# Retention on one Trainium2 core: when GpSimd prepares the next attention's buffers

## The chip, the cores and the metric

The kernel runs on one core of one Trainium2 chip. The core has five engines that run side by side and meet only at semaphores: TensorE (PE in the profile), VectorE (DVE), ScalarE (ACT), GpSimd (POOL) and SyncE (SP), which here only issues transfers. The metric is the device time of one execution in microseconds, the median of several runs. Three runs before the change took 1232.62, 1233.42 and 1237.57 us.

## The reference

Two decoder layers work on 64 sequences of 64 tokens of width 128, so 4096 tokens. Each layer is three sublayers, each added to its input after a layer norm:

```
x = x + state_space(norm(x))          # layer 0
x = x + attention(norm(x), context)
x = x + mixture_of_experts(norm(x))
x = x + retention(norm(x))            # layer 1
x = x + projected_attention(norm(x), context)
x = x + mixture_of_experts(norm(x))
```

The change lies in the retention, 8 heads with keys of 64 and values of 128:

```
q, k = rotary(x @ Wq.T), rotary(x @ Wk.T)       # per head
v, g = x @ Wv.T, x @ Wg.T
scores = (q @ k.T) * 64**-0.5 * decay[head]     # causal, no softmax
o = scores @ v
o = (o - mean(o)) * rsqrt(var(o) + 1e-5) * gn_weight + gn_bias
out = (o * silu(g)) @ Wo.T
```

The attention after it reads keys and values of the context, which were projected at the start of the program and lie in SBUF as kT and v_twice.

## The kernel before

The program is a row of phases, each one block with a barrier at its end. The tokens stay in SBUF as X, 32 tiles of 128 tokens. `layers` (L2083) runs the retention phase between the first mixture of experts and the attention a1.

`retention_phase` (L989) handles one tile per step. Each engine's instructions are written out by hand in `step(i, k)`, and `skewed` (L42) issues them: the first four steps (eight on ACT) are peeled, with step numbers known as Python integers, then comes a hardware loop of four steps per turn, then the last steps, in which only late stages are live. A `between` callback, where given, is issued after the peeled steps. Different stages of different tiles share a step, so the work of a tile spreads over about five steps.

The way of tile m through the engines, in brackets the line:

- ACT normalises the tile into xn (L1211). PE transposes it (L1309), ACT copies it out as the part x_high (L1200), DVE forms the rest x_low (L1155).
- PE makes q and k of all heads (L1232 to L1236), then v with the same lines. DVE multiplies q and k by cosines into qk (L1118), and their swapped halves by sines into turned (L1129). POOL adds turned to qk (L1073): this ends the rotary embedding.
- PE transposes qk (L1266) once POOL has added. ACT copies the transposes (L1187) and v (L1193). PE forms the scores (L1302), DVE multiplies them with the decay table (L1143), PE forms the gates of a pair of tiles (L1243 to L1245) and the mixed values (L1339), ACT applies Silu to the gates (L1206).
- ACT squares the mixed values (L1182), DVE sums them into var (L1107, L1109), POOL raises var to the power -0.5 into rstd (L1070), DVE scales (L1136), PE transposes (L1329), DVE and ACT apply gn_w and gn_b (L1162, L1219), DVE multiplies with the gates (L1101), PE projects with wo (L1278), DVE adds the result to X (L1123).

PE issues in program order: after q and k of tile 1 the next instruction in its queue is the transpose of qk of tile 0, which waits for POOL.

Ahead of the steps stand these parts:

- SP issues six table loads, cos, sin, decay, wo, gn_w and gn_b, which count on the semaphore `loaded` (L1049). Then `setup.sync` (L622) issues the weights of the next attention and, when `k_cleared` says that POOL has cleared the key buffer, 16 transfers (L614) that fill it from kT.
- `RowStatistics` (L127): DVE computes mean and variance of all tiles' rows, POOL makes their rstd in three lots, of 8, 12 and 12 tiles (L158).
- POOL then waits for all three lots, and prepares the next attention's buffers: `clear_keys` (L640) zeroes one buffer k_diag, `clear_values` (L644) zeroes two buffers v_diag, fills `ones` and sets the columns of ones, and `spread_values` (L657), called twice, copies v_twice into v_diag with two products each (L665). Only then comes POOL's step 0.
- ACT, PE and DVE wait for all six tables before their first step, at L1170, L1227 and L1090.

Of the kernel before, what the change touches and what calls it, by code (L numbers as in the profile page):

```python
# [988 lines left out]
def retention_phase(g, setup, weights):  # L989
# [6 lines left out]
    with ExitStack() as ctx:  # L996
# [32 lines left out]
        N, UNROLL = TILES, 4  # L1029
# [13 lines left out]
        with nc.Block() as block:  # L1043
# [8 lines left out]
            @block.gpsimd  # L1052
            def _(pool):
                pool.memset(minus_half[:], -0.5).then_inc(S["half_set"], 1)
                statistics.gpsimd(pool)
                pool.wait_ge(statistics.rstd_ready, len(statistics.LOTS) - 1)
                for k in range(setup.early):
                    setup.clear_keys(pool, k)
                setup.clear_values(pool)
                for j in range(2):  # L1060
                    setup.spread_values(pool, j, j)
                pool.wait_ge(S["half_set"], 1)

                def step(i, k):
                    s = UNROLL * i + k
                    m, b = s - 2, k % 2
                    if live(m, N):
                        pool.wait_ge(S["var_ready"], m + 1)
                        need(pool, S["normed_ready"], m - 1)
                        pool.tensor_tensor(rstd[b][:], var[b][:], minus_half[:], ALU.pow).then_inc(S["rstd_ready"], 1)  # L1070
                    if live(s, N):
                        pool.wait_ge(S["turned_ready"], s + 1)
                        pool.tensor_tensor(qk[k % 2][:], qk[k % 2][:], turned[k % 2][:], ALU.add)\  # L1073
                            .then_inc(S["qk_ready"], 1)
                skewed(pool, N, 2, step, UNROLL)

            @block.vector
            def _(dve):
# [8 lines left out]
                statistics.vector(dve)  # L1087
                dve.wait_ge(statistics.rstd_ready, 1)
                shifts(slice(0, FIRST))
                dve.wait_ge(S["loaded"], 16 * 6)  # L1090

                def step(i, k):

# [17 lines left out]
                    m, b = s - 1, (k - 1) % 2  # L1111
                    if live(m, N):

                        dve.wait_ge(S["qk_in_psum"], m + 1)
                        need(dve, S["qkT_in_psum"], m - 1)
                        src = ps_qk[:].rearrange("p (a e) -> p a e", e=R_KEY)
                        fold = lambda ap: ap.rearrange("p q h e -> p (q h) e")
                        dve.tensor_tensor(fold(qk[b][:]), src,  # L1118
                                          cos[:].unsqueeze(1).to_broadcast([P, 2 * H, R_KEY]), ALU.mult)
# [47 lines left out]

            @block.scalar
            def _(act):
                act.wait_ge(S["loaded"], 16 * 6)  # L1170
                act.wait_ge(S["shift_ready"], 1)

                def step(i, k):

                    first, nearest = UNROLL * i + k, k
                    ahead, place = first - 1, (k - 1) % UNROLL
                    s, k = first - 2, (k - 2) % UNROLL
                    m = s - 2
                    if live(m, N):
                        act.wait_ge(S["mixed_in_psum"], m + 1)  # L1180
                        need(act, S["sum_ready"], m)
                        nc.scalar.activation(square[:], heads(ps_o[:]), ACT.Square).then_inc(S["square_ready"], 1)  # L1182
                    m, b = s - 1, (k - 1) % 2
                    if live(m, N):
                        act.wait_ge(S["qkT_in_psum"], m + 1)
                        need(act, S["scores_in_psum"], m - 1)
                        nc.scalar.activation(qkT[b][:], ps_t[:].rearrange("p (q h t) -> p q h t", q=2, t=P),  # L1187
                                             ACT.Copy).then_inc(S["qkT_ready"], 1)
                    if live(s, N):
                        need(act, S["mixed_in_psum"], s - 1)  # L1190
                        for half in (1, 0):
                            act.wait_ge(S["v_in_psum"], 2 * s + 2 - half)
                            nc.scalar.activation(v[k % 2][:, HP * half:HP * half + HP, :],  # L1193
                                                 heads(ps_vg[:, 512 * half:512 * half + 512]), ACT.Copy)\
                                .then_inc(S["v_ready"], 1)
                    if live(ahead, N):
                        act.wait_ge(S["xnT_in_psum"], ahead + 1)
                        need(act, S["gate_in_psum"], ahead - 2 - place % 2)
                        which, cols = pair(place)
                        nc.scalar.activation(x_high[which][:, cols], ps_qk[:, 0:P], ACT.Copy)\  # L1200
                            .then_inc(S["high_ready"], 1)
                    m, half = s - 1, (k - 1) % 2
                    if live(m, N):
                        act.wait_ge(S["gate_in_psum"], m + 1)
                        need(act, S["gated_ready"], m - 2 - half)
                        nc.scalar.activation(gate[((k - 1) // 2) % 2][:, 4 * half:4 * half + 4, :],  # L1206
                                             ps_vg[:].rearrange("p (h t) -> p h t", t=2 * P), ACT.Silu)\
                            .then_inc(S["gate_ready"], 1)
                    if live(first, N):
                        need(act, S["xnT_in_psum"], first - 1)  # L1210
                        nc.scalar.activation(xn[nearest % 2][:], g.X[:, first, :], ACT.Identity,  # L1211
                                             bias=shift[:, bass.ds(first, 1)], scale=g.rstd[:, bass.ds(first, 1)])\
                            .then_inc(S["xn_ready"], 1)
                    m = s - 2
                    if live(m, N):
                        act.wait_ge(S["normedT_in_psum"], m + 1)
                        need(act, S["out_in_psum"], m - 1)
                        for h in range(DVE_HEADS, H):
                            last = nc.scalar.activation(gated[k % 2][:, h, :].rearrange("p (r t) -> p r t", r=2),  # L1219
                                                        of_head(ps_t, h), ACT.Identity,  # L1220
                                                        bias=gn_b[:, h:h + 1], scale=gn_w[:, h:h + 1])
                        last.then_inc(S["affine_act"], 1)
# [1 line left out]

            @block.tensor
            def _(pe):
                pe.wait_ge(S["loaded"], 16 * 6)  # L1227

                def product(out, k, high, low, before_last=None):

                    which, cols = pair(k)
# [16 lines left out]
                def step(i, k):  # L1248
# [21 lines left out]
                        last.then_inc(S["qkT_in_psum"], 1)  # L1270
                    m, b = s - 3, (k - 3) % 2
                    if live(m, N):
                        pe.wait_ge(S["gated_ready"], m + 1)
                        pe.wait_ge(S["gate_ready"], m + 2 if live(s, N) else min(m + 2, N))
                        if not live(s, N):
# [891 lines left out]
```

## Time and profile before

| What | Value |
| --- | --- |
| Median of three runs | 1233.42 us (1232.62 to 1237.57) |
| Profiled execution, span from first to last instruction | 1231.9 us |
| PE busy | 1109.7 us, 90% of the span |
| DVE busy | 812.4 us, 66% |
| ACT busy | 647.4 us, 53% |
| POOL busy | 585.3 us, 48% |
| Mean granted clock of TensorE | 0.955 of full speed |
| Retention phase | from 496.1 to about 853 us of the span |

The profile gives one profiled execution, and its own time is known only as that span. Times in rows are counted from the start of the span. "x3" is a count of instructions merged into one row, whose duration is then that of the whole run of them. A bracket says how long the engine stood idle before the row and what ended that idle time. The granted clock is given as a share of full speed: 1.00 is TensorE's level of 2.4 GHz, 0.50 the level of 1.2 GHz.

### The profile page before, as it was taken

The numbers are of one execution on the slowest core, as the hardware profiler recorded it, in microseconds if no ns is written. First come the engines' busy times: TensorE is split into PE (matmuls) and PEld (weight loads), VectorE is DVE, ScalarE is ACT, GpSimd is POOL, SyncE is SP. The second block draws the span as 40 slices with busy tenths as digits, with TensorE's granted clock in tenths as the row PEclk, the third lists the DMA queues.
The fourth block names the chain that finished last, engine by engine and source line by source line (L and its number), as shares of the span: only waits on it lengthen the run. The fifth ranks groups of instructions, "written<-read, shape, count | busy, mean of one in ns | idle before, by whom it ended". The sixth has DMA issues, their size and how long they took to land. (4 is left out here: it accounts for less than half of the span.)

```text
span 1231.9 us, 31355 instructions
## 1 busy us (share of the span) xinstructions
PE 1109.7 (90%) x11494; PEld 935.9 (76%) x11494; DVE 812.4 (66%) x1786; ACT 647.4 (53%) x1175; POOL 585.3 (48%) x600
## 2 busy tenths in 40 slices
PE   6979998999999999499999999996899878999970
PEld 4766666789999877388888888885577678899970
DVE  6867997843322434378888888884688766666762
ACT  5416774844566542166666666652688620366630
POOL 5771233025666573733333333333244325677775
PEclk9989999999999999699999999998999979899995
DMA  7023220102223311100000000000111060133242
GB/s 200 10 78 126 65 60 16 61 15 59 71 75 84 118 50 29 41 2 1 0 0 0 0 0 0 0 1 1 19 20 19 6 229 16 55 87 84 84 129 62
DMA packets 59536, 60.78 MB, mean 49 GB/s; under 512 B 12240, under 2 KB 48720, under 8 KB 58928
## 3 DMA queue, kind: packets, MB, share of 16 engines
q1 hardware_dynamic: 49904, 41.63, 11.3%
q0 software_dynamic: 8640, 17.71, 5.7%
q8 instruction: 60, 0.98, 0.3%
q14 instruction: 36, 0.29, 0.1%
q10 hardware_dynamic: 896, 0.17, 0.1%
HBM read 41.77 MB, written 15.60 MB: 47 GB/s over the span
## 5 line engine op out<-in xcount | busy, mean ns | idle before, releaser
L1657 POOL DMA_INDIRECT f_xn<-f_xn_rows,f_source x142 | 137.8, 971 | 41.9 <-issue 41.0
L2048 PE MATMUL f_bank<-f_xT,f_w_tile 128*128 128x128 f32 x1136 | 152.8, 279 | 0.0
L2059 PE MATMUL f_bank<-f_w_down,f_hidden 128*128 x1136 | 150.4, 276 | 0.0
L2048 PEld LDWEIGHTS f_bank<-f_xT,f_w_tile 128*128 128x128 f32 x1136 | 141.0, 195 | 0.0
L2059 PEld LDWEIGHTS f_bank<-f_w_down,f_hidden 128*128 128x128 f32 x1136 | 138.9, 193 | 0.0
L1070 POOL TENSOR_TENSOR ret_rstd<-ret_var,ret_minus_half 128x8 f32<-128x8 f32 x32 | 52.7, 1647 | 173.3 <-DVE ret_var L1109 173.3
L1668 POOL DMA_INDIRECT f_hot_row<-f_slots_y,f_slots x112 | 108.3, 967 | 33.5 <-issue 33.2
L905 PEld LDWEIGHTS a_mixed_psum<-a_v_diag,a_probT 128*64 128x64 f32 x2048 | 66.6, 139 | 59.9 <-ACT a_probT L857 43.7
L767 POOL TENSOR_TENSOR X<-X,a_mixed 128x128 f32<-128x128 f32 x64 | 29.2, 456 | 160.8 <-DVE a_mixed L800 160.3
L808 DVE TENSOR_REDUCE a_top<-a_scores 128x16 f32<-128x1024 f32 x64 | 78.4, 1225 | 36.7 <-PE a_scores L890 35.7
L1942 ACT ACTIVATE f_w_tile<-f_w_up 128x512 f32 x142 | 87.6, 619 | 28.4 <-DVE f_owner L1841 26.8
L857 ACT ACTIVATE a_probT<-a_probT_psum 128x1024 f32<-128x1024 f32 x64 | 65.5, 1024 | 57.5 <-PE a_probT_psum L916 57.5
L1073 POOL TENSOR_TENSOR ret_qk<-ret_qk,ret_turned 128x1024 f32<-128x1024 f32 x32 | 76.2, 2384 | 25.2 <-DVE ret_turned L1129 25.1
L1952 ACT ACTIVATE f_hidden<-f_before_gelu 128x512 f32<-128x512 f32 x71 | 44.8, 631 | 72.0 <-DVE f_before_gelu L1871 72.0
L1886 DVE COPY f_y_out<-f_bank 128x128 f32<-128x128 f32 x71 | 20.7, 292 | 91.7 <-PE f_bank L2059 91.7
L811 DVE TENSOR_TENSOR a_prob<-a_scores,a_top 128x1024 f32<-128x1024 f32 x64 | 78.4, 1225 | 2.2
L905 PE MATMUL a_mixed_psum<-a_v_diag,a_probT 128*64 128x18 f32 x2048 | 72.1, 213 | 7.8 <-ACT a_probT L857 5.7
L1952 ACT ACTIVATE f_hidden<-f_bank 128x512 f32<-128x512 f32 x71 | 42.4, 597 | 64.7 <-PE f_bank L2048 64.7
L916 PE MATMUL a_probT_psum<-ident,a_prob 128*128 128x128 f32 x512 | 70.5, 281 | 5.9 <-ACT a_prob L831 5.9
L1278 PE MATMUL ret_ps<-ret_wo,ret_gated 128*128 128x128 f32 x512 | 67.0, 286 | 4.9 <-DVE ret_gated L1101 4.8
L831 ACT ACTIVATE a_prob<-a_prob 128x1024 f32<-128x1024 f32 x64 | 67.1, 1048 | 6.2 <-DVE a_shift L784 3.3
L1193 ACT ACTIVATE ret_v<-ret_ps 128x512 f32<-128x512 f32 x64 | 38.3, 598 | 58.6 <-PE ret_ps L1236 58.2
(304 smaller groups left out, 2785.8 us busy)
## 6 DMA issues: line engine op xcount, KB each, us to landing
f_slots_y<-f_y_out SPq DMA_DIRECT2D x70, 128.0 KB, 2.2
a_v_rows<-in_ctx SPq DMA_DIRECT2D x16, 256.0 KB, 3.9
f_xn_rows<-f_xn SPq DMA_DIRECT2D x16, 256.0 KB, 6.8
f_w_up<-in_f_up SPq DMA_DIRECT2D x1, 2560.0 KB, 8.6
f_w_down<-in_f_down SPq DMA_DIRECT2D x1, 2560.0 KB, 15.6
f_xn<-f_xn_rows,f_source POOLq DMA_INDIRECT x142, 2.5
X<-in_x SPq DMA_DIRECT2D x4, 512.0 KB, 5.9
kv_ctxT<-in_ctxT SPq DMA_DIRECT2D x8, 256.0 KB, 5.5
```

The lines of the kernel that those rows point to most:

```text
L808: dve.tensor_reduce(top[b][:], bank_s[b][:], AXIS.X, ALU.max).then_inc(S["top_ready"], 1)
L811: dve.tensor_tensor(prob[b][:], bank_s[b][:], top[b][:].unsqueeze(2).to_broadcast([P, HEADS, SEQ]), ALU.subtract)\
L831: nc.scalar.activation(prob[b][:], prob[b][:], ACT.Exp, scale=1.0 / math.sqrt(HEAD))\
L905: last = pe.matmul(bank_o[64 * row:64 * row + 64, 18 * hp:18 * hp + 18], probT[b][:, hp, 64 * row:64 * row + 64], v_diag[octet][:, 2 * (tu ...
L916: last = pe.transpose(bank_t[:, hp, :], prob[b][:, 2 * hp:2 * hp + 2, :].rearrange("p h t -> p (h t)"), g.ident[:])
L1073: pool.tensor_tensor(qk[k % 2][:], qk[k % 2][:], turned[k % 2][:], ALU.add)\
L1657: pool.indirect_dma_start(out=x_in[:, s % RING, :], out_offset=None, in_=xn_rows[:, :], in_offset=bass.IndirectOffsetOnAxis(ap=source[:, s ...
L1668: pool.indirect_dma_start(out=rows[m % len(rows)][:, t, n, :], out_offset=None, in_=slots_y[0:whole[part] * P, :], in_offset=bass.Indirect ...
L1942: nc.scalar.activation(w_tile[s % W_RING][:].unsqueeze(1), w_up[:, bass.ds(expert + E0, 1), :], ACT.Copy)\
L1952: nc.scalar.activation(hidden[m % 3][:].rearrange("p j t -> p (j t)"), before_gelu[m % 3][:].rearrange("p j t -> p (j t)") if biased else ...
L2048: last = pe.matmul(bank_h[m % 3][:, j * P:(j + 1) * P], w_tile[m % W_RING][:, j * P:(j + 1) * P], xT[m % 3][:], start=True, stop=True)
L2059: last = pe.matmul(bank_y[m % 2][:, 0:D].unsqueeze(1), hidden[m % 3][:, j, :], w_down[:, bass.ds(expert + E0, 1), j, :], start=(j == 0), s ...
```

## The change

GpSimd's preparation of the next attention's buffers leaves its place ahead of the steps. `clear_keys` is issued after POOL's step 1, `clear_values` after step 2, the first `spread_values` after step 3, and the second behind the peeled steps, in front of the loop. The order is now pow and add of a step first, then the piece. A wait of POOL for its own `qk_ready` stands ahead of each `spread_values`, and the wait for all lots of rstd is gone. The waits for the six tables move: on DVE to its first rotary product, on ACT to its first affine step (L1216 ff.), on PE to its first projection with wo (L1273 ff.). No instruction other than waits is added or removed.

```diff
             def _(pool):
                 pool.memset(minus_half[:], -0.5).then_inc(S["half_set"], 1)
                 statistics.gpsimd(pool)
-                pool.wait_ge(statistics.rstd_ready, len(statistics.LOTS) - 1)
-                for k in range(setup.early):
-                    setup.clear_keys(pool, k)
-                setup.clear_values(pool)
-                for j in range(2):
-                    setup.spread_values(pool, j, j)
                 pool.wait_ge(S["half_set"], 1)
+
+                def set_up(s):
+
+                    if s == 1:
+                        for k in range(setup.early):
+                            setup.clear_keys(pool, k)
+                    elif s == 2:
+                        setup.clear_values(pool)
+                    elif s >= 3:
+                        pool.wait_ge(S["qk_ready"], min(s + 1, UNROLL))
+                        setup.spread_values(pool, s - 3, s - 3)
...
+                    if isinstance(i, int) and i == 0:
+                        set_up(s)
-                skewed(pool, N, 2, step, UNROLL)
+                skewed(pool, N, 2, step, UNROLL, between=lambda: set_up(UNROLL))
...
                 shifts(slice(0, FIRST))
-                dve.wait_ge(S["loaded"], 16 * 6)
...
+                        if isinstance(m, int) and m == 0:
+                            dve.wait_ge(S["loaded"], 16 * 6)
                         dve.wait_ge(S["qk_in_psum"], m + 1)
...
             def _(act):
-                act.wait_ge(S["loaded"], 16 * 6)
                 act.wait_ge(S["shift_ready"], 1)
...
+                        if isinstance(m, int) and m == 0:
+                            act.wait_ge(S["loaded"], 16 * 6)
                         act.wait_ge(S["normedT_in_psum"], m + 1)
...
             def _(pe):
-                pe.wait_ge(S["loaded"], 16 * 6)
-
...
+                        if isinstance(m, int) and m == 0:
+                            pe.wait_ge(S["loaded"], 16 * 6)
                         pe.wait_ge(S["gated_ready"], m + 1)
```

## Rows read from the trace of the kernel before

**Rows 1.** The list of waits between 496 and 862 us: who waited, total, times, longest

```profile
PE ret_ps L1266 <- POOL ret_qk L1073: 6.7, 1, 6.7
...
PEld ret_ps L1278 <- DVE ret_gated L1101: 7.2, 9, 3.3
```

**Rows 2.** Busy time by stretch: PE, PEld, DVE, ACT, POOL, then granted clock, DMA

```profile
560.00:640.00 80.00, 79.98 (x961) 67.36 (x961) 66.90 (x119) 49.69 (x88) 30.97 (x16) 1.00 0.00 0
```

**Rows 3.** Timeline of POOL from 496 us: start, duration, what, [idle before]

```profile
497.39 6.16 POOL L158 TENSOR_TENSOR rstd<-var,minus_half 128x8 f32<-128x8 f32 x3 [1.11 <-DVE var L148]
503.60 3.51 POOL L642 MEMSET a_k_diag<- 128x4096 f32 x1
507.05 2.06 POOL L648 MEMSET a_v_diag<- 128x1152 f32 x2
...
510.71 5.22 POOL L665 TENSOR_TENSOR a_v_diag<-v_twice,a_ones 64x512 f32<-64x512 f32 x4
516.00 4.65 POOL L1073 TENSOR_TENSOR ret_qk<-ret_qk,ret_turned 128x1024 f32<-128x1024 f32 x2
528.55 1.65 POOL L1070 TENSOR_TENSOR ret_rstd<-ret_var,ret_minus_half 128x8 f32<-128x8 f32 x1 [7.90 <-DVE ret_var L1109]
530.89 2.39 POOL L1073 TENSOR_TENSOR ret_qk<-ret_qk,ret_turned 128x1024 f32<-128x1024 f32 x1 [0.68 <-DVE ret_turned L1129]
538.36 1.65 POOL L1070 TENSOR_TENSOR ret_rstd<-ret_var,ret_minus_half 128x8 f32<-128x8 f32 x1 [5.08 <-DVE ret_var L1109]
540.89 2.39 POOL L1073 TENSOR_TENSOR ret_qk<-ret_qk,ret_turned 128x1024 f32<-128x1024 f32 x1 [0.88 <-DVE ret_turned L1129]
548.60 1.65 POOL L1070 TENSOR_TENSOR ret_rstd<-ret_var,ret_minus_half 128x8 f32<-128x8 f32 x1 [5.33 <-DVE ret_var L1109]
```

**Rows 4.** Timeline of ACT, its first instruction of the retention

```profile
501.68 0.49 ACT L1211 ACTIVATE ret_xn<-X,ret_shift,rstd 128x128 f32<-128x128 f32 x1 [16.91 <-DMA ret_gn_b<-in_ret_gn_b]
```

**Rows 5.** Timeline of DVE over the same start and three later steps

```profile
499.09 0.18 DVE L1080 SCALAR_TENSOR_TENSOR ret_shift<-mean,rstd 128x8 f32<-128x8 f32 x1 [1.85 <-POOL rstd L158]
...
507.64 1.28 DVE L1129 TENSOR_TENSOR ret_turned<-ret_ps,ret_sin 128x512 f32<-128x512 f32 x2
...
512.90 1.28 DVE L1129 TENSOR_TENSOR ret_turned<-ret_ps,ret_sin 128x512 f32<-128x512 f32 x2
...
545.87 1.22 DVE L1101 TENSOR_TENSOR ret_gated<-ret_gated,ret_gate 128x1024 f32<-128x1024 f32 x1 [0.64 <-DVE ret_gated L1162]
...
550.87 1.21 DVE L1136 TENSOR_TENSOR ret_normed<-ret_ps,ret_rstd 128x1024 f32<-128x1024 f32 x1
```

**Rows 6.** Timeline of PE: end of q and k of tile 1, then transposes and scores

```profile
511.32 0.40 PE L1236 MATMUL ret_ps<-ret_wqk_high,ret_x_low 128*128 128x512 f32 x1
518.40 1.97 PE L1266 MATMUL ret_ps<-ident,ret_qk 128*128 128x128 f32 x8 [6.67 <-POOL ret_qk L1073]
...
522.12 0.69 PE L1302 MATMUL ret_ps<-ret_qkT 64*64 64x64 f32 x32
...
526.95 1.03 PE L1266 MATMUL ret_ps<-ident,ret_qk 128*128 128x128 f32 x8
...
529.53 0.70 PE L1302 MATMUL ret_ps<-ret_qkT 64*64 64x64 f32 x32
```

**Rows 7.** Busy time by stretch, two us each, columns as in rows 2

```profile
506.00:508.00 2.00, 2.00 (x8) 1.55 (x6) 1.50 (x2) 0.26 (x1) 2.00 (x2) 0.62 0.00 0
508.00:510.00 2.00, 0.69 (x3) 0.14 (x1) 1.21 (x3) 1.53 (x4) 1.89 (x5) 1.00 0.12 22
...
514.00:516.00 2.00, 0.00 (x0) 0.00 (x0) 0.18 (x1) 0.00 (x0) 1.87 (x2) 0.59 0.13 25
...
520.00:522.00 2.00, 2.00 (x8) 1.48 (x6) 0.00 (x0) 1.50 (x2) 0.65 (x1) 0.71 0.00 0
```

**Rows 8.** Timeline of PE where it enters the loop of the next attention

```profile
876.86 0.30 PE L882 MATMUL a_xT_psum<-ident,a_xn 128*128 128x128 f32 x1 [1.04 <-issue]
```

**Rows 9.** The 16 spreads of this setup: min, median, max in ns, first and last start

```profile
L665 POOL TENSOR_TENSOR a_v_diag<-v_twice,a_ones x16: 1248/1256/1263, 510.7 to 960.9; 64x512 f32<-64x512 f32 x16
```

## The prediction

> **What bounds the kernel now.** I read three views. The busy times by stretch say what paces the retention: between 560 and 640 us PE is busy for 79.98 of 80 us at granted clock 1.00 [rows 2]. A steady step takes some 10.1 us, as POOL's repeating power shows (538.36 to 548.60) [rows 3], and PE fills it. So nothing inside the steady steps is to be had by moving POOL's work. But the phase is a chain of 32 such steps, so whatever delays PE's first steps moves all later ones, and with them the end of the program.
>
> The waits name that delay: PE waits once, 6.7 us, for POOL's first rotary add [rows 1]. The timelines show why. DVE has turned tile 0 ready at 507.64 + 1.28 = 508.92 [rows 5], but POOL is preparing the next attention from 503.60 to 510.71 + 5.22 = 515.93, and its first two adds start at 516.00, each 2.33 [rows 3]. PE had ended q and k of tile 1 at 511.32 + 0.40 = 511.72, sits idle, and starts the transposes at 518.40 [rows 6]. One step ahead, ACT's first instruction starts at 501.68, ended by the landing of gn_b, a table that this instruction does not read [rows 4]; the shift that it does read is ready at 499.09 + 0.18 = 499.27 [rows 5].
>
> **The start, tables waited for later.** ACT starts one semaphore hop after 499.27. The hop from POOL's add (516.00 + 2.33 = 518.33) to PE (518.40) is 0.07 [rows 3, 6], so I put xn of tile 0 at 499.35, earlier by **2.33 us**. X, rstd of the first eight tiles and the weights are in SBUF by then. DVE needs the tables first: its sines end at 508.92, and with the cosines ahead of them (two rows of at most 1.3 us each) its first product starts about 2.4 us earlier, 506.5, thus 504.2 after the change, which is still 2.5 behind 501.68, when all six tables lie there. The moved waits on ACT and PE stand at steps 20 us later and cost nothing. Everything up to q and k of tile 1 moves with this: last matmul ends at 509.39, turned 0 is ready at 506.59, turned 1 at 514.18 - 2.33 = 511.85.
>
> **The start, POOL free.** POOL ends the rstd lots at 503.55 and now waits for turned 0. It adds from 506.67 to 509.0 and PE can start the transposes at 509.1, earlier than the 509.39 at which it gets free. So the idle **6.67 us** [rows 6] goes entirely, and what is late next is PE itself.
>
> **The clock.** In that idle time the granted clock falls (0.59 in 514 to 516) and is back only in the middle of 520 to 522 [rows 7]. From transposes to scores PE then takes 522.12 - 518.40 = 3.72 us, one step later, at full clock, 529.53 - 526.95 = 2.58 [rows 6]. Without the idle time I take the second: **1.14 us** less. The bounds: nothing, if the clock falls all the same, and somewhat more than 1.14, if its first rise comes earlier. It first rose between 506 and 508, some 4 us after q and k began, and the second time under 3 us after PE resumed [rows 7]; the same 1.3 us earlier at the first rise would save about half of that, 0.65, as a matmul at the low level takes twice as long. Between the two bounds the row of 508 to 510 decides: PE is busy for only 0.69 of 2 us there and keeps 1.00, and after the change no longer gap than that one is left.
>
> **The moved pieces.** I keep the old axis; all times after the change are about 10.2 earlier. Keys: add 1 ends at 511.93 + 2.33 = 514.3, the memset takes 3.51, so POOL is free at 517.8. The first power, due at 528.55 - 10.2 = 518.35, has 0.5 us to spare. Its 16 key transfers start 10 us later on SP's queue, which holds nothing else, 340 us ahead of their use. Values: on the old axis add 2 ends at 530.89 + 2.39 = 533.28, the pieces from 507.05 to 510.71 take 3.66, end 536.94, and the next power is due at 538.36: 1.4 to spare. Spreads: add 3 ends at 540.89 + 2.39 = 543.28, four products take 5.22 with their waits, and a hop for the wait on qk_ready makes 548.6, against the next power at 548.60: nothing to spare [rows 3]. But that power ends at 550.25 and DVE takes it at 550.87 [rows 3, 5], so 0.6 us of lateness is free. The second spread stands in front of POOL's loop, whose entry cost no row shows. Below, it is nothing; above, the nearest row is PE entering another loop, 1.04 us of issue [rows 8]. I take nothing, since POOL has so few instructions, and keep 1.04 - 0.6 = 0.4 us for the range.
>
> **A rule against it.** Beside four products of spread DVE multiplies gated by gate (545.87, 1.22 us) [rows 5], both from SBUF, and in the kernel before POOL is idle there. The spreads take 1248 to 1263 ns wherever they stand in the program [rows 9], also inside the next attention beside a busy DVE, though its products there read PSUM. I therefore charge nothing, and carry a collision as a rival.
>
> The Trainium skill, "SBUF — State Buffer", section "Who interferes with whom", says that a DVE instruction with two SBUF inputs and a GpSimd instruction that reads SBUF exclude each other for a whole instruction. By that rule one of the two would wait here; no row of this trace has such a pair to test it, and it says that the memsets, which only write, do not collide with it.
>
> **The sum.** 2.33 + 6.67 + 1.14 = 10.1 us; the chained starts (509.3 + 2.58 = 511.9 for the scores against 522.12) give 10.2, as matmuls overlap a little. I take 10.2: 1231.9 - 10.2 = 1221.7 for the profiled execution. The median of the runs stands 1.5 above that span, so **1223.2 us**.
>
> **Rivals.**
> *A collision at the spreads.* DVE's gate product waits for a product of POOL, up to 1.26, or POOL waits 1.22 and its power is late. PE waits for that DVE product in nine steps already, so it has no slack [rows 1]; the price is about 1.2 us, 1224.4. For: the overlap in time and zero slack. Against: no stretched spread in 16.
> *Given back later.* The phases behind run with stretches at the low clock, and one of three runs took 4.1 us more than the median with the same program. If the earlier work meets a longer low stretch, 1223.2 + 4.1 to + 8 = 1227 to 1231. Against: this is noise that the median mostly removes.
> *The add is not what holds PE.* If PE at 518.40 waited for something that ends with POOL's work only by chance, the 2.33 of the tables would be all, 1231.1, or nothing. Against: ACT's copies, DVE and the weights are done long before, and PE starts 0.07 behind the first add.
> *Slower: TensorE keeps the low clock.* The first q and k start 2.3 us earlier after a long idle, and if the first steps, with their gaps, do not raise the clock, eight transposes take 1.97 in place of 1.03 [rows 6], a factor of 1.9, so a step of 10.1 us costs 9 more. It decides from one whole step on; with two steps the time is 1223.2 + 18 = 1241. Against: the gap of 508 to 510 at 1.00 [rows 7].
>
> **How the numbers follow.** 0.70 for the forecast; 0.15 for the collision; 0.07 for given back; 0.05 for the add that holds nothing; 0.03 for the low clock. The low end: 0.65 for an earlier rise and 0.8 for the lowest run against the median, 1221.7, and 0.5 for what my hops leave open: 1221.2. The high end: collision 1.2, loop entry 0.4, and most of the 4.1 that one run of three lay above the median: 1228. Some 2 in 10 lie outside. A change of 0.5%, 6.2 us, is about what a measurement of this kernel can tell from none. Faster by more (under 1227.3): the first two and a third of the third, 0.87. Within: the rest of the third and the fourth, 0.10. Slower: 0.03.
>
> **What the profile after would show.** ACT's first xn within 0.1 us of the shift; PE's wait for POOL's add gone; the transposes of qk 0 at 509.1 to 509.4 in 1.03 us and no fall of the clock before them; the first scores near 511.9; memset of keys between the second add and the first power; POOL's third power within 0.1 us of its var, and DVE's scaling not waiting for POOL; from there the old step of 10.1 us; the retention ended 10.2 earlier. I am wrong if the steady step is longer, if DVE's gate product is longer than 1.23 beside a spread, or if a later phase is longer by more than 1 us.

## The result, and the profile after

Seven runs of the changed kernel took 1219.51 to 1230.96 us, median **1225.33**; seven of the kernel before 1232.62 to 1237.57, median 1234.87. The ratio is 0.9921, 95% interval 0.9902 to 0.9940: 9.5 us or 0.8% faster. Two further sets on other chips gave 1224.89 against 1235.39 (0.9916, 0.9887 to 0.9945) and 1225.56 against 1234.76 (0.9931, 0.9911 to 0.9951). The profiled execution took 1221.82 us with a span of 1220.0, one of the shorter ones, so its 11.9 us less than the span of before flatter the change.

The page of the kernel after, engines and busy time; nearly the same work stands in a shorter span:

```profile
PE 1109.4 (91%) x11494; PEld 935.5 (77%) x11494; DVE 812.2 (67%) x1786; ACT 646.8 (53%) x1175; POOL 586.6 (48%) x600
```

A phase begins where POOL fills minus_half (L153), so its starts cut the span into phases. All tables in this text count a phase from there.

| Phase, us | before, three profiles | after, three profiles |
| --- | --- | --- |
| state space | 84.71, 84.72, 85.01 | 86.45, 84.68, 85.24 |
| attention a0 | 124.33, 123.08, 121.84 | 123.15, 124.44, 123.25 |
| experts 0 | 286.37, 286.45, 286.41 | 286.33, 286.45, 286.38 |
| **retention** | **357.64, 358.45, 358.71** | **348.46, 349.18, 350.12** |
| attention a1 | 132.93, 130.58, 134.41 | 130.56, 133.98, 133.63 |
| experts 1, to the end | 245.2, 244.7, 244.7 | 244.3, 242.8, 244.5 |

The first number of each is the profile shown here, the others are from the repeats among the experiments. The means of the retention are 358.27 and 349.25, 9.0 us apart. The other phases differ by up to 3.8 us between executions of one program (their sums, in the mean of three, by 0.3 between the two kernels), which is why the medians of the whole cannot judge a term of one microsecond; below, the starts and lengths inside the retention do that.

The timelines of DVE and ACT at its start, for the row of ACT [rows 4] and the first of DVE [rows 5]: ACT follows the shift, not the tables.

```profile
499.62 0.18 DVE L1087 SCALAR_TENSOR_TENSOR ret_shift<-mean,rstd 128x8 f32<-128x8 f32 x1 [1.85 <-POOL rstd L158]
...
499.83 0.49 ACT L1218 ACTIVATE ret_xn<-X,ret_shift,rstd 128x128 f32<-128x128 f32 x1 [14.53 <-DVE ret_shift L1087]
```

The timeline of PE, for [rows 6]. The transposes have no bracket, so no wait, take 1.04 in place of 1.97, and the scores come 2.58 behind them. The phase starts at 496.67, so they stand 13.02 us into it against 22.25 before.

```profile
509.46 0.40 PE L1243 MATMUL ret_ps<-ret_wqk_high,ret_x_low 128*128 128x512 f32 x1
509.69 1.04 PE L1273 MATMUL ret_ps<-ident,ret_qk 128*128 128x128 f32 x8
...
512.27 0.69 PE L1311 MATMUL ret_ps<-ret_qkT 64*64 64x64 f32 x32
```

The timeline of POOL, for [rows 3]. Keys and values lie between the adds and the powers. The four spreads take 6.22 in place of 5.22, and the third power starts at 540.07, 1.5 us after DVE's var was ready at 538.57; before, it followed its var by 0.18.

```profile
507.15 2.37 POOL L1078 TENSOR_TENSOR ret_qk<-ret_qk,ret_turned 128x1024 f32<-128x1024 f32 x1 [3.08 <-DVE ret_turned L1137]
512.39 2.38 POOL L1078 TENSOR_TENSOR ret_qk<-ret_qk,ret_turned 128x1024 f32<-128x1024 f32 x1 [2.87 <-DVE ret_turned L1137]
514.71 3.51 POOL L642 MEMSET a_k_diag<- 128x4096 f32 x1
518.71 1.65 POOL L1075 TENSOR_TENSOR ret_rstd<-ret_var,ret_minus_half 128x8 f32<-128x8 f32 x1 [0.49 <-DVE ret_var L1115]
521.04 2.38 POOL L1078 TENSOR_TENSOR ret_qk<-ret_qk,ret_turned 128x1024 f32<-128x1024 f32 x1 [0.69 <-DVE ret_turned L1137]
523.36 2.06 POOL L648 MEMSET a_v_diag<- 128x1152 f32 x2
...
528.57 1.65 POOL L1075 TENSOR_TENSOR ret_rstd<-ret_var,ret_minus_half 128x8 f32<-128x8 f32 x1 [1.61 <-DVE ret_var L1115]
531.03 2.38 POOL L1078 TENSOR_TENSOR ret_qk<-ret_qk,ret_turned 128x1024 f32<-128x1024 f32 x1 [0.81 <-DVE ret_turned L1137]
533.49 6.22 POOL L665 TENSOR_TENSOR a_v_diag<-v_twice,a_ones 64x512 f32<-64x512 f32 x4
540.07 1.65 POOL L1075 TENSOR_TENSOR ret_rstd<-ret_var,ret_minus_half 128x8 f32<-128x8 f32 x1 [0.36 <-POOL a_v_diag L665]
```

The same spreads by line (min, median, max in ns), for [rows 9]: one product took 2204 ns.

```profile
L665 POOL TENSOR_TENSOR a_v_diag<-v_twice,a_ones x16: 1253/1260/2204, 533.5 to 950.7; 64x512 f32<-64x512 f32 x16
```

DVE's timeline shows what stood beside it, the gate product, with its usual 1.23, and then the scaling, which waits 0.65 for the late power:

```profile
536.01 1.23 DVE L1107 TENSOR_TENSOR ret_gated<-ret_gated,ret_gate 128x1024 f32<-128x1024 f32 x1 [0.64 <-DVE ret_gated L1170]
...
541.74 1.22 DVE L1144 TENSOR_TENSOR ret_normed<-ret_ps,ret_rstd 128x1024 f32<-128x1024 f32 x1 [0.65 <-POOL ret_rstd L1075]
```

Where the gain went: the first power stands 10.36 us earlier in the phase than before (22.04 against 32.40), the seventh 9.92 (83.23 against 93.15), the last 9.93, and the end 9.18. So 0.44 went between the first and the seventh power, nothing in the steady steps, and 0.75 at the drain, the last steps of the phase, in which PE has gaps. There one more projection (PE's product with wo) ran at the low level of the clock. First PE's last two projections of the kernel after, then of the kernel before:

```profile
830.90 3.60 PE L1287 MATMUL ret_ps<-ret_wo,ret_gated 128*128 128x128 f32 x16 [1.88 <-DVE ret_gated L1107]
...
840.02 3.79 PE L1287 MATMUL ret_ps<-ret_wo,ret_gated 128*128 128x128 f32 x16 [2.91 <-DVE ret_gated L1107]
```

```profile
840.31 2.05 PE L1278 MATMUL ret_ps<-ret_wo,ret_gated 128*128 128x128 f32 x16 [1.88 <-DVE ret_gated L1101]
...
848.75 3.72 PE L1278 MATMUL ret_ps<-ret_wo,ret_gated 128*128 128x128 f32 x16 [2.91 <-DVE ret_gated L1101]
```

### The profile page after: what moved, and what is told of

Same layout as the page of the kernel before. It is cut to its first block and busy times, and to the rows that moved or that the text cites. A ratio compares the mean times of both kernels' runs of the same rounds, so it can differ in the third digit from the quotient of the medians.

```text
span 1220.0 us, 31356 instructions
## 1 busy us (share of the span) xinstructions
PE 1109.4 (91%) x11494; PEld 935.5 (77%) x11494; DVE 812.2 (67%) x1786; ACT 646.8 (53%) x1175; POOL 586.6 (48%) x600
## 3 DMA queue, kind: packets, MB, share of 16 engines
HBM read 41.77 MB, written 15.60 MB: 47 GB/s over the span
```

## The experiments

### Tables alone

```diff
                 shifts(slice(0, FIRST))
-                dve.wait_ge(S["loaded"], 16 * 6)
...
+                        if isinstance(m, int) and m == 0:
+                            dve.wait_ge(S["loaded"], 16 * 6)
                         dve.wait_ge(S["qk_in_psum"], m + 1)
```

The same on ACT and PE.

> Only the table waits move, GpSimd's preparation stays ahead of the steps. Theory of the two waits in series: ACT's first xn follows the shift by 0.2 us or less, so q and k of tile 1 end 2.3 us earlier, but PE then waits 9.0 us in place of 6.7 for GpSimd's first add, and the transposes start at the same distance (22.3 us) from the start of the phase; the retention keeps its 357.6 us within 0.3 and the time stays within 1 us of before. Rival, that the table wait is worth its 2.3 us by itself: the transposes start 20.0 us after the start of the phase and the retention takes 355.3 us.

Measured: 1235.22 us, median of ten, against 1235.39; ratio 0.9998 (0.9982 to 1.0014). The retention took 358.17. PE's timeline:

```profile
522.14 1.97 PE L1266 MATMUL ret_ps<-ident,ret_qk 128*128 128x128 f32 x8 [9.11 <-POOL ret_qk L1073]
```

The phase starts at 499.89, so this is 22.25 us into it, exactly as before, with an idle time of 9.11 in place of 6.67. The 2.4 us that the start gains go into the wait for POOL: this half of the change alone is worth nothing. The retention is 0.5 us longer than I had put, because the scores follow the transposes by 4.15 and not 3.72; the clock that comes back later does this in the repeats of the kernel before too, below.

### GpSimd's pieces alone

```diff
-                for k in range(setup.early):
-                    setup.clear_keys(pool, k)
...
+                skewed(pool, N, 2, step, UNROLL, between=lambda: set_up(UNROLL))
```

POOL's part is that of the change, whole; the waits for the tables stay where they were.

> Only GpSimd's preparation moves, all three engines still wait for the six tables at their start. Theory: the transposes of tile 0 follow q and k of tile 1 without a wait, 15.5 us after the start of the phase, at the high clock; the retention is shorter than before by 6.7 + 1.1 = 7.8 us less some 0.4 for the late power at the loop's entry, 7.4. Rival, that the add is not what holds PE: the transposes stay at 22.3 us.

Measured: 1227.54 us against 1235.39; ratio 0.9929 (0.9901 to 0.9957). The retention took 350.10, 7.54 less than before. The transposes, in a phase that starts at 499.90, stand 15.48 us into it, without a wait:

```profile
515.38 1.04 PE L1273 MATMUL ret_ps<-ident,ret_qk 128*128 128x128 f32 x8
```

So POOL's first add did hold PE. Once POOL is out of the way, the tables are worth another 15.48 - 13.02 = 2.46 in the profile above. The two parts are in series, and only the second frees the first. Against the two repeats of the changed kernel below the tables are worth less: 1.3 at the transposes, and 0.9 to 1.0 at the first power, which stands at 24.50 here and at 23.53 and 23.58 there.

### The clock alone

```diff
+                def warm(out, count):
+                    for _ in range(count):
+                        pe.transpose(out, g.ident[:], g.ident[:])
...
+                        if isinstance(m, int) and m == 0:
+                            warm(ps_t[:, 0:P], 50)
                         pe.wait_ge(S["qk_ready"], m + 1)
```

> The kernel before, with 50 transposes of the identity that nobody reads, issued by PE where it waits for GpSimd's first add. Theory that the clock was worth 1.14 us: the granted clock does not fall between 512 and 518 us, the transposes of tile 0 start at the same time and take 1.03 in place of 1.97, the first scores follow them by 2.6 in place of 3.7, and the retention is shorter by 1.1 us. Rival, that the low clock there is hidden by ACT's copies: the retention stays at 357.6 us.

Measured: the retention took 356.59, 1.05 less; the whole 1234.56 against 1235.39, ratio 0.9996 (0.9978 to 1.0014), too small to see there. PE's timeline, in a phase that starts at 496.55:

```profile
518.84 1.09 PE L1272 MATMUL ret_ps<-ident,ret_qk 128*128 128x128 f32 x8 [1.31 <-POOL ret_qk L1073]
521.48 0.69 PE L1308 MATMUL ret_ps<-ret_qkT 64*64 64x64 f32 x32
```

The transposes start at 22.29, where they did, and the scores follow by 2.64 in place of 3.72. The first power is 1.03 earlier. Against this profile of before the term of 1.14 holds to 0.1.

### The changed kernel again, twice

> The changed kernel once more. Its start of the retention should repeat to 0.1 us (transposes of tile 0 at 13.1 us after the start of the phase, a product of the spreads stretched by about 1 us to 2.2, third power 1.5 us late). Theory that the wide spread of its runs comes from TensorE's clock where PE has gaps, at the drain of the retention and in the last mixture of experts: the phases that differ between the two profiles of this kernel are those with a granted clock under 1.00, by up to 2 us each, and the steady steps agree within 0.1. Rival, that the change made the steps themselves vary: the steady steps differ.

> The changed kernel a third time, beside e9_filled on the same chip. Theory that its start has two courses: either the clock rises late, near 507 us, and stays (transposes of tile 0 at 13.0 us after the start of the phase) or it rises early, near 504, and falls again in the gap before q and k of tile 1 (14.2). The retention is 348.5 to 349.2 us and e9_filled is shorter than it by about 4 us there, by 3 to 6 in the whole. Rival, that the time between the two medians is noise of other phases: e9_filled within 1 us of this kernel.

Measured: 1224.89 and 1225.56 us. The distances of the steady powers agree to 0.02 with the first profile, one product of the spreads was stretched each time (2182 and 2164 ns), and the third power again stood 1.5 behind its var. But the start did not repeat to 0.1: the transposes stand 14.20 and 14.12 us into the phase in place of 13.02. PE's timeline of the second profile, in a phase that starts at 496.31:

```profile
510.51 1.35 PE L1273 MATMUL ret_ps<-ident,ret_qk 128*128 128x128 f32 x8
...
513.41 0.69 PE L1311 MATMUL ret_ps<-ret_qkT 64*64 64x64 f32 x32
```

The busy times by stretch say why (columns as in rows 2). First the profile of the first run:

```profile
506.00:508.00 2.00, 1.31 (x4) 0.45 (x2) 1.16 (x3) 1.33 (x4) 0.85 (x1) 0.78 0.00 0
508.00:510.00 2.00, 1.81 (x9) 1.48 (x10) 0.25 (x2) 0.19 (x1) 1.52 (x1) 1.00 0.00 0
```

And the second profile:

```profile
504.00:506.00 2.00, 1.67 (x7) 1.00 (x5) 1.78 (x3) 0.89 (x2) 0.00 (x0) 0.92 0.00 0
506.00:508.00 2.00, 0.52 (x2) 0.36 (x3) 0.93 (x3) 0.96 (x3) 1.21 (x1) 0.93 0.00 0
508.00:510.00 2.00, 2.00 (x5) 1.62 (x6) 0.00 (x0) 0.00 (x0) 1.14 (x1) 0.50 0.00 0
```

In the first the clock rose late, near 507, and stayed at 2.4 GHz. In the second it rose early, near 504, v of tile 0 ended sooner, PE stood idle until tile 1, and the clock fell back to 1.2 GHz. The course with the early rise is 1.2 us longer, and 1.5 by the first power (23.53 against 22.04). The third profile took the second course. So the start of the changed kernel has two courses. At its drain the last projection but one took 3.60, 2.05 and 3.68 us in the three.

The phases that differ most between the first two profiles differ in their clock, as expected: a1 took 130.56 us at a mean granted clock of 0.984 and 133.98 at 0.946. This is 3.4 us, more than the 2 I had put. In the third profile the retention took 350.12, longer than the 349.2 I had put.

### The kernel before again, twice

> The kernel before, unchanged, for a second profile. Of the profiles so far the last but one projection of the retention ran at the low clock (3.6 us) in five of seven kernels with the pieces moved and in none of the three with the pieces in front (2.05 us), where the retention took 356.6 to 358.2. Theory that this is a draw of the clock that the change does not touch: it should come at 3.6 in at least one of the two further profiles of this kernel, with a retention 0.7 to 0.9 us longer. Rival, that the changed kernel favours it: 2.05 in both. The start should repeat: transposes of tile 0 at 22.25 after the start of the phase, first power at 32.4 to 32.8.

> The same once more. Theory of the draw: the last but one projection at 3.6 us here or in b_again. Rival: 2.05 in both. The clock's course at the start of the phase may be either, but the transposes of tile 0 stay at 22.25, since POOL holds them.

One run each, 1230.53 and 1233.57 us. The transposes stand at 22.24 and 22.27, held by POOL whatever the clock does ahead of them. But the clock came back later than in the first profile: PE's timeline of the first repeat, in a phase that starts at 494.99,

```profile
517.23 1.97 PE L1266 MATMUL ret_ps<-ident,ret_qk 128*128 128x128 f32 x8 [6.81 <-POOL ret_qk L1073]
521.69 0.81 PE L1302 MATMUL ret_ps<-ret_qkT 64*64 64x64 f32 x32
```

has the scores 4.46 us behind the transposes, not 3.72, and the first power at 33.24; the other repeat has 4.46 and 33.33. The clock term of the idle time is thus 1.14 to 1.9. Over three profiles of each kernel the first power moved from 32.99 to 23.05 in the mean, 9.9 us.

At the drain the last projection but one took 2.05 in both. That is now five profiles of five with the pieces in front, and 3.6 to 3.7 in five of the seven profiles with the pieces moved and nothing added at the drain. My theory of a mere draw predicted a slow one here and found none; with so few profiles it is likely, not shown, that the changed kernel meets the low clock there more often. Why it should, no run shows.

### The pieces spaced

```diff
+                for k in range(2):
+                    pool.memset(v_diag[k][:], 0.0).then_inc(SS["v_cleared"], 1)
+                pool.memset(ones[:], 1.0).then_inc(SS["v_cleared"], 1)
...
                 def set_up(s):
+                    if s == 0:
+                        pool.wait_ge(SS["v_cleared"], 3)
+                        pool.wait_ge(S["qk_ready"], 1)
...
-                    elif s == 2:
-                        setup.clear_values(pool)
-                    elif s >= 3:
-                        pool.wait_ge(S["qk_ready"], min(s + 1, UNROLL))
-                        setup.spread_values(pool, s - 3, s - 3)
+                    elif s in (2, 3):
+                        pool.wait_ge(S["qk_ready"], s + 1)
+                        setup.spread_values(pool, s - 2, s - 2)
...
-                skewed(pool, N, 2, step, UNROLL, between=lambda: set_up(UNROLL))
+                skewed(pool, N, 2, step, UNROLL)
```

> The changed kernel with the pieces placed where GpSimd idles and DVE does not multiply two SBUF tensors: the memsets of the values in front of step 0, the columns of ones behind step 0, the keys behind step 1, one spread behind step 2 and one behind step 3, none in front of the loop. Theory that the third power was late because a product of the spreads met DVE's gate product and because they stood before the loop: no product of the spreads over 1.3 us, the third power some 42.0 us after the start of the phase in place of 43.4, DVE's scaling does not wait for it, and the later powers are 0.4 us earlier than in the changed kernel; retention shorter by 0.4. Rival, that the loss comes from the loop's entry on another engine: later powers unchanged.

Measured: 1227.66 us, six runs between 1222.11 and 1231.33, ratio 0.9927 (0.9899 to 0.9955): not to be told from the changed kernel. POOL's timeline, in a phase that starts at 495.72:

```profile
532.70 2.60 POOL L665 TENSOR_TENSOR a_v_diag<-v_twice,a_ones 64x512 f32<-64x512 f32 x2
537.94 1.65 POOL L1085 TENSOR_TENSOR ret_rstd<-ret_var,ret_minus_half 128x8 f32<-128x8 f32 x1 [2.65 <-DVE ret_var L1125]
```

No product over 1281 ns, and the third power at 42.22 in place of 43.40, waiting for DVE and not DVE for it. From the first to the seventh power it takes 60.94 against 61.19 in the changed kernel and 60.75 before: only 0.25 of the 0.44 came back. The other 0.19 lies between the first and the second power (10.05 against 9.81 before), where DVE's timeline has a new delay:

```profile
524.23 0.92 DVE L1097 SCALAR_TENSOR_TENSOR ret_shift<-mean,rstd 128x24 f32<-128x24 f32 x1
```

The small product of shifts, two SBUF tensors of 24 columns, takes 0.18 in the kernel before and 0.92 here, beside the spread that now lies behind step 2. The collision had moved with the spread.

### Reads and writes exchanged

```diff
                     if s == 1:
-                        for k in range(setup.early):
-                            setup.clear_keys(pool, k)
+                        setup.clear_values(pool)
                     elif s == 2:
-                        setup.clear_values(pool)
-                    elif s >= 3:
-                        pool.wait_ge(S["qk_ready"], min(s + 1, UNROLL))
-                        setup.spread_values(pool, s - 3, s - 3)
+                        pool.wait_ge(S["qk_ready"], 3)
+                        for j in range(2):
+                            setup.spread_values(pool, j, j)
+                    elif s == 3:
+                        for k in range(setup.early):
+                            setup.clear_keys(pool, k)
```

> The changed kernel with another order: values cleared behind step 1, both spreads behind step 2, keys cleared behind step 3. Theory that DVE with two SBUF inputs shuts out only reads of GpSimd: of the four products one meets DVE's gate product of tile 0 and takes about 2.2 us in place of 1.26, while the memset of the keys, which lies over the gate product of tile 1, stays at 3.51; the second power is late by about 0.9, the third on time. Rival, that the stretch came from something in front of the loop: no product over 1.3. Rival, that any GpSimd work beside that DVE product stretches: the memset takes about 4.5.

One run, 1227.58 us; retention 349.92, with the start's second course (14.21). The spreads by line, min, median and max in ns:

```profile
L665 POOL TENSOR_TENSOR a_v_diag<-v_twice,a_ones x16: 1253/1260/2217, 526.2 to 956.4; 64x512 f32<-64x512 f32 x16
```

POOL's timeline, the memset of the keys:

```profile
536.46 3.52 POOL L642 MEMSET a_k_diag<- 128x4096 f32 x1
```

DVE's timeline, with the gate products of tiles 0 and 1:

```profile
527.93 0.92 DVE L1088 SCALAR_TENSOR_TENSOR ret_shift<-mean,rstd 128x24 f32<-128x24 f32 x1
528.77 1.21 DVE L1108 TENSOR_TENSOR ret_gated<-ret_gated,ret_gate 128x1024 f32<-128x1024 f32 x1
...
538.90 1.23 DVE L1108 TENSOR_TENSOR ret_gated<-ret_gated,ret_gate 128x1024 f32<-128x1024 f32 x1 [0.26 <-DVE ret_gated L1171]
```

The stretch moved with the spreads, away from the loop's entry, and the memset, which lies over the gate product of 538.90, kept its 3.52. Both engines waited in turn: DVE's shifts for a product of POOL (0.92), then a product of POOL for DVE's gate product (2.22). The second power came 1.2 late (34.61 against 23.57 + 9.86 = 33.43), more than the 0.9 I had put; the third, 0.18 behind its var, was on time.

This is the rule that the prediction had kept as a rival. The Trainium skill, "SBUF — State Buffer", section "Who interferes with whom", gives DVE instructions with two SBUF inputs and GpSimd's reads one shared port, and leaves GpSimd's pure writes out. The rows agree: the spread reads SBUF and met both DVE instructions with two SBUF inputs, and the memset, which only writes, met one without a delay. So the engines of this core do not meet at semaphores alone, as the first section has it.

The trace of before already held such pairs, outside the retention. This is the timeline of DVE and then of POOL in the state space: the product of shifts of 24 columns takes 1.23 there in place of 0.18, beside a product of POOL.

```profile
28.22 1.23 DVE L321 SCALAR_TENSOR_TENSOR ssm_shift<-mean,rstd 128x24 f32<-128x24 f32 x1 [2.33 <-POOL rstd L158]
```

```profile
28.15 1.26 POOL L460 TENSOR_TENSOR ssm_part_cos<-ssm_part_cos,ssm_part_sin 128x512 f32<-128x512 f32 x1
```

One pair did not collide. DVE's shift of 8 columns [rows 5] lies inside POOL's second lot of rstd, a power with two SBUF inputs, 499.04 to 501.31 within the first row of [rows 3]. It took its usual 0.18, and the lot 2.27, where the other lots of 12 tiles take 2.26 to 2.34, in every profile of this case. Why a power leaves room where a product does not, no run shows.

### Warm start, drain, and the filled gap

Three kernels add transposes of the identity, with the `warm` of above, into PSUM places whose content nobody needs at that moment. The first is the changed kernel with 18 at PE's start; the second has the spaced pieces too, and more at the drain; the third also fills the gap of the start. The diff is that of the third: its 5 and 10 are the third's alone, its 14 and 12 the second's too, its 18 in all.

```diff
...
+                            warm(ps_t[:, 0:P], 5)
                         pe.wait_ge(S["low_ready"], s + 1)
...
+                            warm(ps_t[:, 0:P], 10)
                         pe.wait_ge(S["xn_ready"], ahead + 1)
...
+                            warm(ps_qk[:, 0:P], 14)
                         pe.wait_ge(S["gated_ready"], m + 1)
...
+                            warm(ps_qk[:, 0:P], 12)
                         pe.wait_ge(S["normed_ready"], m + 1)
...
+                warm(ps_t[:, 0:P], 18)
```

> The changed kernel with 18 transposes of the identity that nobody reads, issued by PE at the start of the phase, where it waits for ACT's first xn. Theory that the start chain now holds q and k of tile 0 at the low clock, and that the moment of the clock's rise is what varied by 1.2 to 1.5 us between the two profiles of the changed kernel: six matmuls of 0.23 in place of 0.43, so the transposes of tile 0 start 11.8 us after the start of the phase in place of 13.0, and the retention is shorter by 1.2. Rival, that the clock is not raised in time by so few transposes: 13.0 to 14.2 again.

> Pieces spaced as in e4_spaced, 18 transposes at the start as in e6_warm_start, and 14, 12 and 14 more that nobody reads in the waits of PE at the end of the retention (before the last two projections and the last transposes of the normed values). Theory: 0.4 and 1.2 from the start as there, and at the end the last projection takes 2.05 in place of 3.78 because the clock does not fall, so the retention takes 345.2 us against 348.5 of the changed kernel, and the whole some 3 us less than the changed kernel, about 1222 us. Rival, that the clock falls there for another reason: the last projection stays at 3.7 and the retention at 346.9.

> As e8_drain, with 10 more transposes that nobody reads before the transposes of xn of tile 1 and 5 before q and k of tile 1, in the two waits of 1.3 and 0.7 us after which the clock had fallen there. Theory that this gap of PE is what lets the clock fall: no low stretch between 502 and 520 us, q and k of tile 1 take 1.4 us in place of 2.6, the transposes of tile 0 start 11.8 us or less after the start of the phase in 1.03 us and the first scores stand at 14.4, so the retention takes 1.2 us less than in e8_drain, 344.6. Rival, that the fall is not tied to the gap: the transposes start at 12.8 as in e8_drain.

| | transposes of tile 0 | first power | last projection starts, takes | retention | median, us |
| --- | --- | --- | --- | --- | --- |
| after, three profiles | 13.02, 14.20, 14.12 | 22.04, 23.53, 23.58 | 343.35, 3.79 (first) | 348.46, 349.18, 350.12 | 1225.33 |
| warm start | 12.62 | 22.18 | 343.54, 3.78 | 348.65 | 1227.81 |
| and spaced, drain | 12.80 | 22.07 | 342.41, 2.05 | 345.78 | 1223.28 |
| and gap filled | 12.26 | 21.34 | 341.67, 2.05 | 345.05 | 1224.22 |

The warm start did its part and lost most of it again, 12.62 in place of the 11.8 I had expected: q and k of tile 0 ran at full clock, PE then waited 1.3 us for tile 1, and q and k of tile 1 fell to the low level. PE's timeline with the warm start (phase from 496.75) and then with the gap filled (phase from 496.58):

```profile
505.83 0.30 PE L1322 MATMUL ret_ps<-ident,ret_xn 128*128 128x128 f32 x1 [1.30 <-DVE ret_turned L1137]
506.82 0.62 PE L1243 MATMUL ret_ps<-ret_wqk_high,ret_x_high 128*128 128x512 f32 x1 [0.69 <-DVE ret_x_low L1163]
...
509.37 1.57 PE L1277 MATMUL ret_ps<-ident,ret_qk 128*128 128x128 f32 x8
```

```profile
508.84 1.09 PE L1289 MATMUL ret_ps<-ident,ret_qk 128*128 128x128 f32 x8 [0.29 <-POOL ret_qk L1088]
...
511.48 0.69 PE L1329 MATMUL ret_ps<-ret_qkT 64*64 64x64 f32 x32
```

With the gap filled nothing falls, and the scores stand at 14.90 against 15.60 in the better course of the changed kernel and 17.10 in the other. I had expected 11.8 and 14.4: PE now waits 0.29 for POOL's first add, which is the next thing late. So the third kernel's retention is 0.7 us shorter than the second's, and not 1.2; the second's is 345.78, where I had put 345.2. The drain kept the clock as expected, 3.79 to 2.05.

In the whole these kernels cannot be told from the changed one: 1224.22 (eight runs, ratio 0.9930, 0.9907 to 0.9952) beside 1225.56 (six runs, ratio 0.9931) on the same chip, 1.3 us less where I had expected 3 to 6. The second kernel has a ratio of 0.9904 (0.9876 to 0.9932) beside 0.9927 of the spaced pieces on its chip. In the profile of the last the retention is 3.4 to 5.1 us shorter, but a1 and experts 1 together took 380.6 in the last of them and 379.1 in the one before, against 374.9 to 378.1 in the changed kernel and 375.3 to 379.1 in the kernel before. Whether the transposes cause that, or it is the usual difference between executions, is open. None of them is claimed as a faster version.

## Why the prediction was right

Forecast 1223.2 us, between 1221.2 and 1228.0, with 0.87 on faster; measured 1225.33. Of the 2.1 us between, 1.45 is the median of before, which rose from 1233.42 to 1234.87 with four more runs, and 0.7 is gain that was missing: 9.5 in place of 10.2. The profiles, three each, have 9.0 in the retention: 9.9 at the first power, less 0.44 up to the seventh and some 0.5 at the drain. The two parts of the change and their order are as forecast; that the sum came so near is in part luck, as the bullet on the clock says.

- **Tables, 2.33.** ACT started 3.16 us into the phase in place of 5.53: 2.37. Tables alone gave nothing. With the pieces moved they gave 2.46 in the first profile, and 0.9 to 1.3 against the repeats, where the clock took the rest. That both waits must go is as the working has it, since it took them in series. The price of the moved waits, nothing, also held: DVE's first product began at 504.58, as soon as PE's product allowed.
- **The idle time, 6.67.** Gone. PE's wait became 0.2 us in the list of waits, on the weight load alone.
- **The clock, 1.14.** 1.05 when measured by itself, and up to 1.9 by the repeats of the kernel before. But the working also took from one row that the clock would hold across the gap before tile 1 [rows 7], and in the changed kernel this was true in one profile of three. This step failed: one row is one draw. By the mean clocks of the two-microsecond stretches it rose some 5.8 us behind ACT's first instruction in the first profile of before and 7.0 in that of after, and held; in the two repeats of after it rose 4.9 and 5.0 behind it, and fell again. In that course the start gives 1.5 less. The working also put a gain of 0.65 on an earlier rise, and it was a loss. That the repeats of before start later too, by 0.9, hides most of it, and this is luck: 9.9 in the mean against 10.1 to 10.2. The rival of a clock that stays low had the right mechanism, with a price of 1.2 to 1.5 us once and not of 9 per step.
- **Keys and values.** 0.5 and 1.4 to spare were forecast before the first and second power; the idle times are 0.49 and 1.61.
- **Spreads, nothing.** Wrong by 0.44. They took 1.0 us more than before, from one product that DVE's gate product shut out, and 0.36 passed from their end to the power, with the loop's entry in between. So the third power stood 1.5 behind its var in place of 0.18; 0.6 was free, and DVE waited 0.65. The rival had this, at 1.2 us and 0.15. Its price came out smaller because POOL waited and not DVE, and the slack took part of it. The reason for charging nothing, that no row of the trace had such a pair, was a reading that failed: the retention had none, but the state space had one, at 28.22.
- **Given back later.** The drain of the retention took 0.75 in the first profile, with one more projection at the low clock: the mechanism of that rival, in a place that the working had not looked at. It came in two of three profiles of the changed kernel and in none of before, so some 0.5 of the gain went there in the mean; whether the change brings it is not shown.
- **Steady step.** 82.93 to 93.15 before, 73.02 to 83.23 after: 10.2 in both.

## What to carry to other kernels

Work that an engine does for a later phase belongs in its idle times inside the first steps, but price it by who is queued behind it at every place, and move front waits in the order in which they end: the one that ends first is worth nothing alone. Ask of each moved GpSimd piece whether it reads SBUF, and of each DVE instruction beside it whether it has two SBUF inputs; the memset of the keys could lie beside such an instruction without a delay. Before charging nothing for such a pair, search the whole trace for one, and not only the phase that changes. A profile's granted clock in one gap is a single draw: look at a second execution before resting a term on it.

## What the runs showed of the hardware

- GpSimd's product (1.26 us alone) took 2.16 to 2.22 beside a DVE product with both inputs in SBUF, which kept its 1.23; a DVE product of 24 columns took 0.92, and 1.23 in the state space, in place of 0.18 beside GpSimd's product. GpSimd's memset of 128x4096 stayed at 3.52 beside the same DVE product, and its power of 12 columns at 2.27 with a DVE product of 8 columns inside it, at 0.18.
- An earlier rise of TensorE's clock can go with a longer time: with v of tile 0 done sooner PE stood idle longer (busy 0.52 of the 2 us from 506 to 508), the clock fell from 2.4 to 1.2 GHz, and the next products took 0.63 in place of 0.39. Filling that gap with 15 transposes kept the clock, in the one profile taken.
- 0.36 us passed on GpSimd between the last spread and the next instruction where a loop's entry stood between them, and 0.08 in the kernel with reads and writes exchanged, where none did.
